# Second and third state scan of a step joined into one of 1024 columns in the Mamba layer of a two-layer network

## The reference

```python
# 16 images, 32x32 = 1024 tokens, di = 96 channels, D_STATE = 16 states per channel
dt = softplus(einsum('blr,dr->bld', dt_r, dt_w) + dt_b)
A = -exp(A_log)
def step(h, inp):
    dt_t, x_t, B_t, C_t = inp
    da = exp(dt_t[..., None] * A)                               # decay
    h = da * h + (dt_t * x_t)[..., None] * B_t[:, None, :]      # drive
    y = einsum('bdn,bn->bd', h, C_t)
    return h, y
y = scan(step over tokens) + xm * Dp
y = y * silu(z)
```

## Time and profile before

| | before |
|---|---|
| median of 3 executions | 1671.23 us (1666.82 to 1675.09) |
| profiled execution | 1674.63 us |
| its span, first to last instruction | 1672.8 us |
| DVE busy | 1296.3 us, 77% |
| PE busy | 1294.4 us, 77% |
| ACT busy | 1164.9 us, 70% |
| POOL busy | 975.8 us, 58% |

### The profile page before, as it was taken

The page is one execution under the profiler, slowest core; times in us unless marked ns, Lnnn a source line. Parts: engine busy times, 40 slices in busy tenths (PEclk is TensorE's granted clock), DMA queues, the critical chain, the costliest instruction groups (busy, mean ns, idle before and its releaser), DMA issues. The chain is left out here.

```text
span 1672.8 us, 15960 instructions
## 1 busy us (share of the span) xinstructions
PE 1294.4 (77%) x3822; PEld 437.0 (26%) x3822; DVE 1296.3 (77%) x1358; ACT 1164.9 (70%) x1789; POOL 975.8 (58%) x515
## 2 busy tenths in 40 slices
PE   4999657475574478867888888888888888876996
PEld 2344201010010255532222222222222222112563
DVE  1656559789798276730799999999999999994675
ACT  2676358587585277757888888889888888640564
POOL 2400037868679433323988898888888998860000
PEclk8999855555555699978797888888888888555997
DMA  5344330200200233325777777777777776735472
GB/s 156 95 141 134 86 121 1 80 22 2 101 0 25 82 90 98 94 59 124 176 179 175 165 169 175 172 178 178 180 175 172 171 172 154 150 74 112 110 175 66
DMA packets 136563, 200.40 MB, mean 120 GB/s; under 512 B 26733, under 2 KB 68989, under 8 KB 135708
## 3 DMA queue, kind: packets, MB, share of 16 engines
q1 hardware_dynamic: 134246, 196.08, 47.8%
q10 hardware_dynamic: 1798, 2.68, 0.6%
q0 software_dynamic: 448, 0.85, 0.2%
HBM read 145.93 MB, written 53.63 MB: 119 GB/s over the span
## 5 line engine op out<-in xcount | busy, mean ns | idle before, releaser
L1804 DVE TENSOR_TENSOR_SCAN m_h<-m_qa,m_state,m_ub 128x512 f32<-128x512 f32 x384 | 464.1, 1263 | 16.3 <-POOL m_ub L1425 11.3
L1425 POOL TENSOR_TENSOR m_ub<-m_dlb,m_bt 128x1536 f32<-128x1536 f32 x128 | 438.3, 3444 | 17.4 <-DVE m_h L1804 12.7
L1765 ACT ACTIVATE m_qa<-m_dlb,k_a 128x512 f32<-128x512 f32 x384 | 253.5, 681 | 82.1 <-DVE m_h L1804 81.0
L1148 POOL TENSOR_TENSOR b_u<-b_dl,b_z 128x1024 f32<-128x1024 f32 x48 | 125.9, 2624 | 206.2 <-DMA b_z<-scratch_z 159.7
L1618 PE MATMUL m_qc<-m_bcr,k_selc 32*128 32x512 f32 x256 | 165.6, 730 | 95.7 <-DVE m_g L1815 95.5
L1815 DVE TENSOR_TENSOR m_g<-m_h,m_qc 128x1536 f32<-128x1536 f32 x128 | 221.7, 1732 | 6.2 <-issue 2.9
L1635 PE MATMUL m_qy<-m_g,k_seld 128*32 128x512 f32 x768 | 176.7, 774 | 0.0
L984 PE MATMUL b_qb<-b_bc,k_pack_sel 96*128 96x512 bf16 x96 | 78.6, 819 | 108.3 <-DVE b_u L1068 108.3
L1042 ACT ACTIVATE b_qa<-b_dl,b_a 128x512 f32<-128x512 f32 x96 | 65.5, 684 | 91.4 <-DVE b_h L1083 78.7
L1083 DVE TENSOR_TENSOR_SCAN b_h<-b_qa,b_h,b_u 128x512 f32<-128x512 f32 x84 | 108.0, 1286 | 0.1
L1559 PE MATMUL m_qf<-m_cva,k_conv 113*96 113x504 f32 (+1 forms) x192 | 101.7, 671 | 5.0 <-PEq L1179 5.0
(11 more groups left out here) (187 smaller groups left out, 2644.6 us busy)
## 6 DMA issues: line engine op xcount, KB each, us to landing
m_dlb<-scratch_dldu SPq DMA_DIRECT2D x128, 384.0 KB, 10.4
m_bt<-scratch_brow SPq DMA_DIRECT2D x128, 256.0 KB, 5.9
scratch_dldu<-m_dldu SPq DMA_DIRECT2D x32, 384.0 KB, 3.2
scratch_z<-a_z SPq DMA_DIRECT2D x24, 256.0 KB, 6.0
b_z<-scratch_z SPq DMA_DIRECT2D x3, 2048.0 KB, 8.7
scratch_y<-b_yrow SPq DMA_DIRECT2D x12, 512.0 KB, 2.8
c_y<-scratch_y SPq DMA_DIRECT2D x16, 384.0 KB, 3.4
scratch_gate<-m_gt SPq DMA_DIRECT2D x32, 192.0 KB, 3.6
```

The source lines that it names most:

```text
L1148: nc.gpsimd.tensor_tensor(by_column(u[s][:], col), by_column(dl[s][:], col), seen(z[:], col, piece), ALU.mult).then_inc(u_ready, 1)
L1425: nc.gpsimd.tensor_tensor(ub[k % 3][:], dlb[u % 2][:, J:2 * J, :], bcast(bt[u % 2][:, n, :], J), ALU.mult).then_inc(ub_ready, 1)
L1765: nc.scalar.activation(q_a[:, j, :], dlb[u % 2][:, j, :], ACT.Exp, scale=G["a1"][:, j, n:n + 1]).then_inc(da, 1)
L1804: nc.vector.tensor_tensor_scan(h[k % 3][:, j, :], q_a[:, j, :], ub[k % 3][:, j, :], state[:, k % NS, j:j + 1], ALU.mult, ALU.add).then_inc ...
```

## The change

The second and third scan of a step become one scan over 1024 columns. The third group must not go on from the second, so its first decay is to be zero: that column of `m_qa` is set to zero once, and the third exponential writes the other 511 columns. What the third recurrence would have taken from its carried value, exp(dt·A)·state of the first column, is added to the drive's first column instead. ACT does that in two instructions of one column: an exponential into `m_afirst`, and a multiply-add into `m_ub`. The second waits for the first, for POOL's drive and for an earlier `keep`. The two new semaphores are `carried` and `reset`; the counts of `scanned` (3 a step, now 2) and `da` (3 a step, now 4) are changed where they are waited for.

```diff
@@ gpsimd, drive(k)
                 if k >= 3:
-                    pool.wait_ge(scanned, 3 * (k - 3) + 3)
+                    pool.wait_ge(scanned, 2 * (k - 3) + 2)
+                    pool.wait_ge(carried, k - 2)
@@ sync, load_drive(v)
-                    sp.wait_ge(da, 3 * (4 * (v - 2) + 4))
+                    sp.wait_ge(da, 4 * (4 * (v - 2) + 4))
@@ scalar, decay(k)
                 for j in range(J):
 
                     if k >= 1:
-                        act.wait_ge(scanned, 3 * (k - 1) + j + 1)
-                    nc.scalar.activation(q_a[:, j, :], dlb[u % 2][:, j, :], ACT.Exp,
+                        act.wait_ge(scanned, 2 * (k - 1) + min(j, 1) + 1)
+                    at = 1 if j == J - 1 else 0
+                    nc.scalar.activation(q_a[:, j, at:CH], dlb[u % 2][:, j, at:CH], ACT.Exp,
                                          scale=G["a1"][:, j, n:n + 1]).then_inc(da, 1)
+                first = a_first[:, k % 3:k % 3 + 1]
+                nc.scalar.activation(first, dlb[u % 2][:, J - 1, 0:1], ACT.Exp,
+                                     scale=G["a1"][:, J - 1, n:n + 1]).then_inc(da, 1)
+                start = ub[k % 3][:, J - 1, 0:1]
+                act.wait_ge(ub_ready, k + 1)
+                act.wait_ge(da, 4 * k + 4)
+                if k >= NS // 4:
+                    act.wait_ge(kept, max(k - 3, 0))
+                nc.scalar.activation(start, first, ACT.Identity, scale=state[:, k % NS, J - 1:J],
+                                     bias=start).then_inc(carried, 1)
@@ vector, scans(k)
+            nc.vector.memset(q_a[:, J - 1, 0:1], 0.0).then_inc(reset, 1)
...
-                for j in range(J):
-                    dve.wait_ge(da, 3 * k + j + 1)
-                    nc.vector.tensor_tensor_scan(h[k % 3][:, j, :], q_a[:, j, :], ub[k % 3][:, j, :],
-                                                 state[:, k % NS, j:j + 1], ALU.mult, ALU.add).then_inc(scanned, 1)
+                dve.wait_ge(da, 4 * k + 1)
+                nc.vector.tensor_tensor_scan(h[k % 3][:, 0, :], q_a[:, 0, :], ub[k % 3][:, 0, :],
+                                             state[:, k % NS, 0:1], ALU.mult, ALU.add).then_inc(scanned, 1)
+
+                dve.wait_ge(da, 4 * k + 3)
+                dve.wait_ge(carried, k + 1)
+                pair = [tile[:, 1:J, :].rearrange("p j t -> p (j t)") for tile in (h[k % 3], q_a, ub[k % 3])]
+                nc.vector.tensor_tensor_scan(*pair, state[:, k % NS, 1:2], ALU.mult, ALU.add).then_inc(scanned, 1)
```

More of the change, by code:

```diff
@@ L1372, in mid1_phase @@
         state = m.sb("m_state", [P, NS, J])
+        a_first = m.sb("m_afirst", [P, 3])
         q_a = m.ps("m_qa", [P, J, CH])
@@ L1383, in mid1_phase @@
                 "summed", "corr", "du_ready", "ub_ready", "delta", "scanned", "read", "y_ready"))
+        reset, carried = m.sem("m_reset"), m.sem("m_carried")
         cv_loaded, gt_stored, dldu_stored, dlb_loaded, bt_loaded, y_stored = (
@@ L1770, in keep @@
                     return
-                act.wait_ge(scanned, 3 * k + 3)
+                act.wait_ge(scanned, 2 * k + 2)
                 nc.scalar.activation(state[:, k % NS, :], h[k % 3][:, :, CH - 1], ACT.Identity).then_inc(kept, 1)
@@ L1791, in _ @@
         def _(dve):
+            nc.vector.memset(q_a[:, J - 1, 0:1], 0.0).then_inc(reset, 1)
             dve.wait_ge(zeroed, NZ)
+            dve.wait_ge(reset, 1)
             def scans(k):
@@ L1809, in times_c @@
                     return
-                dve.wait_ge(scanned, 3 * k + 3)
+                dve.wait_ge(scanned, 2 * k + 2)
                 dve.wait_ge(c_mm, k + 1)
```

## The result

| | before | changed |
|---|---|---|
| median | 1669.6 us (4 runs) | 1710.39 us (4 runs, 1702.48 to 1713.08) |
| profiled execution, span | 1674.63, 1672.8 us | 1702.48, 1700.7 us |

The ratio is 1.0232 with a 95% interval of 1.0186 to 1.0279: the change makes the kernel slower by 2.3%, 40.8 us between the medians. The profiled execution of the changed kernel is the shortest of its four and that of before was one of the longer, so the spans differ by only 27.9 us. The phase itself shows more: from the first to the last step's first scan it is 799.5 to 1511.5 before and 795.6 to 1544.7 after, 37 us longer. The other stages were some 9 us shorter in that execution, and the change does not touch them.

The account below looks back on a forecast made before the run. A loop through POOL and ACT was taken as the bound, not DVE. 28 turns × 1.14 us, less 1.1, gave +30.8 on 1674.6, 1705.4; that execution stands 3.4 above the median, so 1702 us, range 1686 to 1713.

Parts of the forecast that it names:

- The bound: Loop through POOL's leg (12.02 us) and ACT's leg (10.08) sets the 22.22 us turn; DVE has 0.28 to spare.
- The long scan: On DVE, the 1024-column scan takes 2.35 us for 2.44, saving 0.09 a step, worth nothing while the loop sets the turn.
- The small instructions: Two one-column ACT instructions add 0.48 us to each group of exponentials; two groups in ACT's leg, +0.96 a turn.
- my dear end of 0.58 a group: High price of the one-column ACT instructions, the second paying for both column operands (0.36 us): 0.58 us a group.
- three dear terms: Dearest case: 0.58 a group, a pair of scans of 2.44 and the window's cover overrun by 0.1: 1714 us.
- a window out of its cover: On ACT ahead of the window, the added delay outgrows the idle time hiding it, by 0.1 us in the dearest case.
- The exponentials that wait together: In ACT's leg, the next group's second exponential waits 0.18 us for the end of the joined scan, once a turn.
- The sum: Over 28 turns: 1.14 us each is 31.9, less 1.1 behind the loop, +30.8 us in all.
- 1.1 us back: Behind the last rounding, about 12 steps set by DVE each save 0.09 us.
- DVE is the bound: Rival: POOL and ACT have slack, so the scans' saving counts; turn 21.58 us, 1652 in all, faster, chance 0.06.
- The second chain: Rival that only the window matters: ACT and DVE alone set a turn of 22.48 us, 1677, no change, chance 0.08.
- The cover of 1.03 us ahead of L1686: ACT's idle time before L1686 just hides the 1.08 us by which the group ahead of the window runs later.

Follow-up runs that it names:

- e1: Kernel before plus only the two one-column ACT instructions behind each group of exponentials, their result read by nobody; 1704.97 us, ratio 1.0189.
- e3: Kernel before with POOL's sum of the taps put ahead of the drive of the same step; 1676.03 us against 1670.46.
- e11: Kernel before with ACT's four last softplus functions put between the first and the other two exponentials of their step; 1679.49 us against 1670.56.
- e2: Changed kernel without its two one-column ACT instructions, leaving out the value carried into the third group of channels; 1673.47 us against 1670.46 for the kernel before.
- e5: Kernel before with one wait changed: the next step's exponential 1 waits for the third scan, as in the changed kernel; 1681.72 us against 1673.42.
- e4: Changed kernel with POOL's sum of the taps put ahead of the drive of the same step; 1708.12 us, ratio to before 1.0199.
- e6: Changed kernel with the carried value added by DVE from SBUF operands, and a unit's four first-column exponentials made by one ACT instruction; 1932.42 us, ratio to before 1.1547.
- e7: The kernel of e6 with POOL's sum of the taps put ahead of the drive; 1938.84 us, ratio to before 1.1592.
- e10: Changed kernel with a unit's four first-column exponentials made by one ACT instruction of 128x4, multiply-adds staying on ACT; 1700.68 us, ratio to before 1.0182.
- e9: Changed kernel with the carried value added by DVE, which reads the first decay from PSUM and then zeroes it; 1710.75 us, ratio to before 1.0249.
- e12: The kernel of e3 with less PE work: the convolution's low part and third column of taps left out; 1696.07 us, 1.3% slower than e3.

## Why the prediction was right

- **The bound.** POOL's L1443 and L1686 on ACT close a loop, DVE at 99% is only 0.26 us a turn behind it: shown. Lengthening ACT's leg alone lengthens every turn by as much (e1), and taking a drive or two exponentials out of it lets the quiet turn fall to 21.95, the 21.94 added up for DVE (e3, e11).
- **The long scan.** 2.35 forecast, 2.33 measured. It gives nothing, since no scan stands in the loop: e2, with the scan and without the small instructions, is as fast as before.
- **The small instructions.** The place was right, the size was off: 0.48 us a group forecast, 0.66 measured. The exponential lasts 0.28 (0.27 forecast). The multiply-add lasts 0.39 (0.27), which fits a price for each of its two operands from a column in SBUF; and it starts 0.09 us behind the end of the first, where I took 0.03 from a pair with one semaphore. With both it lies above my dear end of 0.58 a group. That the time stayed inside the range is in part luck: with 0.66 the prediction's own sum is 28 × 1.50 − 1.1 = +40.9, 1712, a microsecond below the top of 1713. The top had been made of three dear terms, and the other two, a long scan of 2.44 us and a window out of its cover, did not come.
- **The exponentials that wait together.** 0.18 forecast, 0.16 measured; alone (e5) it is 0.21.
- **The sum.** 1.14 us a turn forecast, 1.46 measured between quiet turns; 28 turns give 31.9 and 40.9. Between mean turns it is 1.35, 37.8 us for 28, because the kernel before has some long turns too. Behind the last rounding I expected 1.1 us back; from there to the last step's first scan it is 59.7 us before and 57.4 after. The medians differ by 40.8, the phases of the two profiled executions by 37. That 40.9 and 40.8 meet so closely is chance.
- **The rivals.** That DVE is the bound is excluded by e1. The second chain was a real one, but I had left out POOL's rounding and DVE's L1833 in it and put it at 22.48; e4 shows 23.29 for it. The cover of 1.03 us ahead of L1686 held, with 0.26 left. By the prediction's own numbers, 1.08 us later, it would have been overrun by 0.05; it held because the scans ahead of the window now end 6.77 us behind POOL's rounding (1304.79 − 1298.02), in place of 7.30.
- **What I had not priced:** PE. In the kernel before its stretches at 1.2 GHz mostly fall where they hold nobody up (23 of 28 turns are 22.2). In the kernel before the mean turn is 0.2 us above the quiet one, in the variants, e6 and e7 aside, 0.2 to 0.9. The waits for PE in e3's long turns are shown; that they are also what keeps e11 from being faster I take from its list of waits, which has the same ones, and it was not tested apart. For the other variants it is argued only. In the changed kernel the mean is only 0.08 us above the quiet turn.

No version here beats the kernel before.

## What to carry to other kernels

An engine that is busy 99% need not be the bound: look for the waits that recur once per turn on the other engines, and add up the legs between them; if they give the turn to 0.1 us, that loop is the bound. What is added to a leg then counts in full, from its start to the start of what stands behind it, and what stands in no leg counts nothing as long as no other chain outgrows the loop. What is taken out counts only down to the next bound: e3 took a drive of 3.42 us out of a leg, the quiet turn fell by 0.25, and the time not at all. Before moving a small piece of work to another engine, ask which leg it lands in and where its operands lie: 0.66 us of one-column work in two places cost this kernel 2%, and one column on DVE with two SBUF operands beside a busy POOL cost 15%.

## What the runs showed of the hardware

- ACT, changed kernel, medians: 190 ns with no column operand (`keep`, 128x3), 279 with a scale from SBUF (128x1), 386 with scale and bias from SBUF (128x1; 372 in e10). That is 89 ns for the first and some 100 for the second; the functions differ (Identity, Exp, Identity).
- DVE: a scan of 512 columns 1.27 us, of 1024 columns 2.33; about 2.06 ns a column and 0.2 us fixed.
- DVE with two tensors from SBUF beside POOL (e6): one column took up to 5.95 us, and 0.19 us when one of them lay in PSUM (e9).
- PE: the kernel that gives it less to do was granted the lower clock, 0.74 for 0.86, and took 20 us longer (e12 against e3).
- PE: behind a pause of 2.24 us the granted clock was 0.50, from 1194 to 1197 in the kernel before and from 1153 to 1166 in e3.
